# Attention rows split into f16 halves per head and turned by transposing DMAs per pair of heads

## The chip, the core and the metric

The kernel runs on one core of a Trainium2 chip, in one launch. The metric is the device time of one execution in microseconds (us). Differences in this text are differences of that time. The profile is taken from one execution; its engines are PE (TensorE matmul), PEld (TensorE weight load), DVE (VectorE), ACT (ScalarE), POOL (GpSimd) and SP (SyncE, which issues most DMAs).

## What is computed

Two residual blocks on x of shape (4, 1024, 256). The first is a cross attention whose queries are the normalised x and whose keys and values come from the context rows and the normalised x together, with 16 heads of 64 columns; the second is a layer of eight experts of which the best one is taken for each token. Cut to what matters here:

```python
def _L0_xattn_ref(x, latents, ...):
    x = layer_norm(x, ln_m_g, ln_m_b)            # context, (4, 154, 256)
    lat = layer_norm(latents, ln_l_g, ln_l_b)    # (4, 1024, 256)
    q = lat @ Wq
    k, v = jnp.split(jnp.concatenate([x, lat], axis=1) @ Wkv, 2, axis=-1)
    q, k, v = (split_heads(q), split_heads(k), split_heads(v))
    dots = jnp.einsum('bhid,bhjd->bhij', q, k) * scale
    out = jnp.einsum('bhij,bhjd->bhid', jax.nn.softmax(dots, axis=-1), v)
    return out.transpose(0, 2, 1, 3).reshape(b, m, heads * dim_head) @ Wout

x = x + _L0_xattn_ref(ctx_1024, _layernorm(x), ...)
x = x + _L0_ffn_ref(_layernorm(x), ...)          # top-1 of eight experts
```

## The kernel before

**Precision.** Products that need more than f16 are made from halves: a value is kept as an f16 high half and an f16 low half (the value less its high half), and a product is summed from high x high, high x low and low x high.

**Order of work.** The attention part runs over 64 heads, 16 for each of 4 batches. A head h has ten steps j, one for each tile of up to 128 keys (JT = 10). PE's order is written out by hand. At step j it scores the tile that lies three tiles ahead (`tile_ahead`), makes the small chunks that a table places beside the step (`BESIDE`: the next heads' q/k projections "qk", maxima of scores "rest" and "first", their tails, a "turn" of the maxima, values "v", and in some heads the gate "xt" and "gate" of the batch before or the next batch's columns "z"), and weighs the values with the tile's probabilities (`weigh`), which adds up in `acc`. Chunks go through two PSUM banks `aux[0]` and `aux[1]` in turn; a chunk can start when the chunk two before it has been taken by DVE (`aux_done`). The gate chunks lie beside heads 4 to 11 of batches 1, 2 and 3.

**Engines.** ACT makes the exponentials of each scored tile twice, as f32 (`exponent`) and as the f16 high half (`high_half`). POOL makes the low half (`low_half`, L783) for nine of the ten tiles, and in each head also turns a piece of the expert weights into two halves (L792, L795). DVE takes the chunks (`consume`): for a q/k chunk a cast to `raw[0]` (L1059) and a subtraction to `raw[1]` (L1061), for a maximum a reduction (L1077); it also makes the low half of the last tile, on 32 rows (L1152). After the ten steps, `take_rows(h)` divides the sums in `acc` by their denominators (L1139, L1141).

**SP's queue.** All of SP's DMAs leave in program order: per head the stores and the load of the weight piece, `arrange(h + 2)` (the projected q and k are copied to where the scores read them) when the third q/k chunk is done, `send_max(h + 1)` when the "turn" chunk is done, and `arrange_low(h + 2)`.

**The end of a batch.** `att_rows` holds the divided rows of all 16 heads as f32, 128 rows by 8 tiles by 1024 columns. In `put_out(b)` PE turns a tile of 128 rows by eight f32 transposes through a score bank (L1380), ACT casts the turned tile to its high half (L942), DVE subtracts for the low half (L1181), and PE multiplies the tile with `Wout` in 24 products of 256 columns (L1297, pair by pair, three products each). Tile t + 2 is turned behind tile t's products. For tiles 0 and 1 the first seven pairs are turned before the batch's last rows are there. DVE adds the residual rows (L1114) that SP loads into the two `x_res` buffers, tile t + 2's load behind the addition of tile t, and makes the sums of the next norm. In the last batch the gate's chunks for the same batch stand between the tiles.

Of the kernel before, what the change touches and what calls it, by code (L numbers as in the profile page):

```python
# [339 lines left out]
def attention(nc, x, ctx_in, ln, Wq, Wkv, Wout, x2_dram, gate, W1, W2, split_dram):  # L340
# [12 lines left out]
    with stack:  # L353
# [33 lines left out]
        probs_split = [[sb(f"probs_split{h}{i}", [P, N], F16) for i in range(SPLITS)] for h in range(2)]  # L387
# [4 lines left out]
        att_rows = sb("att_rows", [P, NT, H, DH], F32)  # L392

        att_turn = sb("att_cols", [P, 2, 2, INNER // P, P], F16)
        att_cols = [[att_turn[:, h, i, :, :] for i in range(2)] for h in range(2)]
        x_next = att_turn[:, :, :, :, :].rearrange("p a b k t -> p (a b k t)").bitcast(F32)\
# [20 lines left out]
        staging = att_rows[:, :, :, :].rearrange("p t h d -> p (t h d)")  # L417
# [50 lines left out]
        att_turned = sem("att_turned")  # L468
        att_high = sem("att_high")
        att_low = sem("att_low")  # L470
        res_loaded = [sem(f"res_loaded{i}") for i in range(2)]
# [46 lines left out]
        def bank_of(chunk):  # L518
            return aux[NUMBER[chunk] % 2]
# [30 lines left out]
        EARLY = range(PAIRS - 1)  # L550
        PARTS = [EARLY, range(PAIRS - 1, PAIRS)]
        TURNS = NT + 1

        def turn_bank(t, ks):
            return acc if t == 0 and ks != EARLY else score[(t + 1) % 2]

        def turns_of(b, t, part=1):

            return TURNS * b + (part + 1 if t == 0 else t + 2)

        def last_scored(h, i):

            return (h + 1, 2 - i) if h + 1 < HEADS else (h, JT - 2 + i)

        def columns(ks):
            return slice(ks.start * P, ks.stop * P)
# [31 lines left out]
        def _(sp):  # L598
# [14 lines left out]
            sp.dma_start(x_next, x_rows[1]).then_inc(x_loaded[1], 16)  # L613
# [52 lines left out]

            def send_max(g):

                sp.wait_ge(aux_done, NUMBER["turn", g] + 1)
                sp.dma_start(q_max[g % 2][DH:DH + 1, :], max_row[g % 2][:, :]).then_inc(max_sent, 16)  # L670

            def head(h):
                if h > 0:
                    store_piece(h - 1)
                load_piece(h)
                for step in BESIDE[h]:
                    for chunk in step:
                        if chunk == ("qk", h + 2, QK - 1):
                            arrange(h + 2)
                        elif chunk == ("turn", h + 1):  # L680
                            send_max(h + 1)
                if h + 2 < HEADS:
                    arrange_low(h + 2)
                if h % H == 0 and 2 <= h // H + 1 < B:

                    sp.dma_start(x_next, x_rows[h // H + 1]).then_inc(x_again, 16)

            def put_out(b):
                if b == B - 1:
                    store_piece(HEADS - 1)  # L690

                def store(t):
                    sp.wait_ge(aux_done, NUMBER["out", b, t] + 1)
                    sp.dma_start(x2_rows[b, t], x2_keep[:, t, :]).then_inc(x2_stored[t % 2], 16)

                for t in range(NT):
                    if t >= 2:
                        sp.wait_ge(aux_done, NUMBER["out", b, t - 2] + 1)
                    sp.dma_start(x_res[t % 2], x_rows[b, :, t, :]).then_inc(res_loaded[t % 2], 16)
                    if t >= 1:  # L700
# [20 lines left out]
        def _(pool):  # L721
# [64 lines left out]
            for h in range(HEADS):  # L786
                for j in range(JT):
                    low_half(h, j)
                    if j == PIECE_STEPS[0]:
                        pool.wait_ge(piece_loaded, 16 * (h + 1))  # L790
                        at_least(pool, piece_stored, 2 * 16 * h)
                        nc.gpsimd.tensor_copy(piece_out[0][:, :], piece_in[:, :]).then_inc(piece_high, 1)  # L792
                    elif j == PIECE_STEPS[1]:
                        pool.wait_ge(piece_high, h + 1)
                        nc.gpsimd.tensor_tensor(out=piece_out[1][:, :], in0=piece_in[:, :], in1=piece_out[0][:, :],  # L795
                                                op=ALU.subtract).then_inc(piece_low, 1)
# [7 lines left out]
        def _(act):  # L804
# [55 lines left out]
            def normalise_next(b, t):  # L860

                if t == 0:
                    act.wait_ge(inverse_ready, b)
                    if b >= 2:
                        act.wait_ge(x_again, 16 * (b - 1))
# [70 lines left out]
            def put_out(b):  # L936
                for t in range(NT + 2):
                    if t < NT:
                        for part, ks in enumerate(PARTS if t == 0 else [range(PAIRS)]):
                            act.wait_ge(att_turned, turns_of(b, t, part))  # L940
                            act.sem_inc(act_turns, 1)
                            nc.scalar.activation(att_cols[0][t % 2].rearrange("p k t -> p (k t)")[:, columns(ks)],  # L942
                                                 turn_bank(t, ks)[:, columns(ks)], ACT.Copy).then_inc(att_high, 1)
# [14 lines left out]
        def _(dve):  # L958
# [22 lines left out]
            def rows_of(group):  # L981

                return (x_stage[0], x_stage[1], x_next, x_stage[0], x_stage[1])[group], \
                    C_ROWS if group == 0 else [P] * NT
# [148 lines left out]
            def take_rows(h):  # L1133

                for i in range(2):
# [5 lines left out]
                    nc.vector.tensor_tensor(out=att_rows[:, ts, h % H, :], in0=sums[:, :, 0:DH],  # L1141
                                            in1=recip[:, ts].unsqueeze(2).to_broadcast([P, NT // 2, DH]), op=ALU.mult)\
                        .then_inc(rows_taken, 1)

# [29 lines left out]
            def put_out(b):  # L1174
                steps = output_chunks(b)
                for t in range(len(steps) + 1):
                    if t < NT:
                        for part, ks in enumerate(PARTS if t == 0 else [range(PAIRS)]):
                            high, low = [a[t % 2][:, :, :].rearrange("p k t -> p (k t)")[:, columns(ks)] for a in att_cols]
                            dve.wait_ge(att_high, turns_of(b, t, part))  # L1180
                            nc.vector.tensor_tensor(out=low, in0=turn_bank(t, ks)[:, columns(ks)], in1=high,  # L1181
                                                    op=ALU.subtract).then_inc(att_low, 1)
# [28 lines left out]
        def _(pe):  # L1211
# [31 lines left out]
            def produce(chunk):  # L1243
# [44 lines left out]
                elif kind == "out":  # L1288
                    t = chunk[2]
                    parts = PARTS if t == 0 else [range(PAIRS)]  # L1290
                    for part, ks in enumerate(parts):
                        pe.wait_ge(att_low, turns_of(g, t, part))
                        for k in ks:
                            lhs = [a[t % 2][:, k, :] for a in att_cols]
                            rhs = [w[:, k, :] for w in wo]
                            for i, (m, n) in enumerate(((0, 0), (0, 1), (1, 0))):
                                last = nc.tensor.matmul(bank[:, 0:D], lhs[m], rhs[n], start=(k == 0 and i == 0),  # L1297
                                                        stop=(k == PAIRS - 1 and i == 2))
# [15 lines left out]
                last.then_inc(aux_full, 1)  # L1314

# [19 lines left out]
            def weigh(h, j, i):  # L1335
# [3 lines left out]
                if j == 0:  # L1339
                    at_least(pe, rows_taken, 2 * (h - 1) + i + 1)  # L1340
                    if i == 0:
                        pe.wait_ge(aux_done, NUMBER["v", h // 2, len(VALUE_TILES) - 1] + 1)
                r = key_rows(j)
# [16 lines left out]
            def head(h):  # L1360
                for j in range(JT):
# [6 lines left out]
                    if j == JT - 1 and outputs_behind(h) is not None:  # L1368
                        pe.wait_ge(rows_taken, 2 * h)
                        wait_high(pe, *last_scored(h, 1))  # L1370
                        turn_pairs(0, EARLY).then_inc(att_turned, 1)
# [5 lines left out]
            def turn_pairs(t, ks):  # L1377

                for k in ks:
                    last = nc.tensor.transpose(turn_bank(t, ks)[:, k * P:k * P + P], att_rows[:, t, 2 * k:2 * k + 2, :]  # L1380
                                               .rearrange("p h d -> p (h d)"), ident[:, :])
                return last

            def put_out(b):
                pe.wait_ge(w_low, 7)
                h = H * b + H - 1
                wait_high(pe, *last_scored(h, 0))
                turn_pairs(1, EARLY)
                pe.wait_ge(rows_taken, 2 * H * (b + 1))
                turn_pairs(0, PARTS[1]).then_inc(att_turned, 1)  # L1390
                turn_pairs(1, PARTS[1]).then_inc(att_turned, 1)
                for t, step in enumerate(output_chunks(b)):
# [495 lines left out]
```

## Time and profile before

| | |
|---|---|
| Time, median of 3 runs | 2083.61 us (2081.96 to 2087.18) |
| Profiled execution, span from first to last instruction | 2083.0 us |
| Mean granted TensorE clock in it | 0.982 |
| Busy: PE, DVE, ACT, POOL | 1982.6, 1516.5, 1526.0, 1442.8 us |
| DMA packets | 129585, 140.02 MB |

The time of the profiled execution is known by its span; the median of the runs is 0.6 us above it. Busy times of different engines overlap. PE's matmuls are pipelined, so the step from one start to the next tells more than the duration of one.

### The profile page before, as it was taken

The numbers are of one execution on the slowest core, as the hardware profiler recorded it, in microseconds if no ns is written. First come the engines' busy times: TensorE is split into PE (matmuls) and PEld (weight loads), VectorE is DVE, ScalarE is ACT, GpSimd is POOL, SyncE is SP. The second block draws the span as 40 slices with busy tenths as digits, with TensorE's granted clock in tenths as the row PEclk, the third lists the DMA queues.
The fourth block names the chain that finished last, engine by engine and source line by source line (L and its number), as shares of the span: only waits on it lengthen the run. The fifth ranks groups of instructions, "written<-read, shape, count | busy, mean of one in ns | idle before, by whom it ended". The sixth has DMA issues, their size and how long they took to land. (4 is left out here: it accounts for less than half of the span.)

```text
span 2083.0 us, 63335 instructions
## 1 busy us (share of the span) xinstructions
PE 1982.6 (95%) x25468; PEld 1359.6 (65%) x25468; DVE 1516.5 (73%) x2951; ACT 1526.0 (73%) x2006; POOL 1442.8 (69%) x818
## 2 busy tenths in 40 slices
PE   4999999999999999999999999999999998599997
PEld 1566666667666666676666666766666666467775
DVE  8777777776777777777877777777777774745554
ACT  3688888885888787858888888678888886156664
POOL 3688888883888888838888888568888886023332
PEclk8999999999999999999999999999999999799999
DMA  5222222222222222223222222222222221381110
GB/s 190 50 64 59 56 58 68 56 50 78 72 55 56 56 55 56 58 66 76 63 59 55 56 56 55 59 65 66 61 56 55 56 55 32 95 310 39 43 48 25
DMA packets 129585, 140.02 MB, mean 67 GB/s; under 512 B 45569, under 2 KB 94389, under 8 KB 128149
## 3 DMA queue, kind: packets, MB, share of 16 engines
q1 hardware_dynamic: 125557, 126.58, 23.6%
q0 software_dynamic: 3744, 9.39, 1.5%
q8 instruction: 210, 3.44, 0.7%
q14 instruction: 74, 0.61, 0.1%
HBM read 55.15 MB, written 26.15 MB: 39 GB/s over the span
## 5 line engine op out<-in xcount | busy, mean ns | idle before, releaser
L783 POOL TENSOR_TENSOR probs_split<-probs,probs_split 128x1024 f16<-128x1024 f32 x576 | 1221.7, 2134 | 256.1 <-ACT probs_split L890 246.8
L883 ACT ACTIVATE probs<-score 128x1024 f32<-128x1024 f32 (+1 forms) x640 | 655.5, 1024 | 303.6 <-PE score L1240 296.4
L1077 DVE TENSOR_REDUCE max_parts<-aux 128x1 f32<-128x512 f32 x1024 | 682.8, 687 | 79.0 <-PE aux L1240 71.0
L890 ACT ACTIVATE probs_split<-score 128x1024 f16<-128x1024 f32 (+1 forms) x640 | 654.0, 1022 | 0.0
L1352 PE MATMUL acc<-values,probs_split 128*128 128x65 f16 x5120 | 553.8, 193 | 8.2 <-POOL probs_split L783 8.1
L1356 PE MATMUL acc<-values,probs_split 128*128 128x64 f16 x4608 | 519.0, 194 | 0.0
L1357 PE MATMUL acc<-values,probs_split 128*128 128x65 f16 x4608 | 517.0, 192 | 0.0
L1352 PEld LDWEIGHTS acc<-values,probs_split 128*128 128x128 f16 x5120 | 461.4, 97 | 68.3 <-POOL probs_split L783 11.7
L1240 PE MATMUL score<-q_max,k_low 65*128 65x512 f16 (+1 forms) x1280 | 486.6, 380 | 0.0
L1240 PE MATMUL score<-q_both,k_high 128*128 128x512 f16 (+1 forms) x1280 | 483.9, 378 | 0.9 <-DMA q_max<-max_row 0.5
L1240 PE MATMUL aux<-k_high,q_both 128*128 128x512 f16 (+1 forms) x1536 | 457.9, 332 | 19.0 <-DVE max_parts L1077 7.1
L1356 PEld LDWEIGHTS acc<-values,probs_split 128*128 128x128 f16 x4608 | 425.9, 97 | 74.1
L1357 PEld LDWEIGHTS acc<-values,probs_split 128*128 128x128 f16 x4608 | 427.2, 99 | 0.0
L1240 PEld LDWEIGHTS aux<-k_high,q_both 128*128 128x128 f16 x1536 | 141.8, 98 | 156.1 <-DVE max_parts L1077 41.5
L1240 PE MATMUL aux<-zx,wqk 128*128 128x512 f16 x768 | 191.4, 386 | 2.1 <-DVE zx L1027 2.1
L1059 DVE CAST raw<-aux 128x512 f16<-128x512 f32 (+1 forms) x192 | 108.8, 567 | 94.9 <-PE aux L1240 81.6
L1240 PEld LDWEIGHTS score<-q_max,k_low 65*128 65x128 f16 (+1 forms) x1280 | 127.0, 99 | 68.3 <-issue 0.3
L1240 PEld LDWEIGHTS score<-q_both,k_high 128*128 128x128 f16 (+1 forms) x1280 | 129.9, 101 | 62.7 <-issue 1.4
L1810 PE MATMUL up<-shared,w 128*128 128x128 f16 x1872 | 162.7, 223 | 4.4 <-issue 2.1
L1810 PEld LDWEIGHTS up<-shared,w 128*128 x1872 | 131.3, 99 | 53.3 <-issue 17.7
L1583 POOL DMA_INDIRECT out<-shared,write_i x39 | 39.9, 1022 | 168.1 <-DVE shared L1745 168.1
L1617 ACT ACTIVATE shared<-up,b_cols 128x128 f32<-128x128 f32 x312 | 88.9, 368 | 87.9 <-PE up L1810 87.8
(182 smaller groups left out, 2220.2 us busy)
## 6 DMA issues: line engine op xcount, KB each, us to landing
k_high<-raw SPq DMA_DIRECT2D x128, 147.2 KB, 2.5
q_both<-raw SPq DMA_DIRECT2D x128, 128.0 KB, 2.5
piece_in<-in_L_ffn_W SPq DMA_DIRECT2D x64, 256.0 KB, 3.2
halves<-piece_out SPq DMA_DIRECT2D x128, 128.0 KB, 2.4
k_low<-raw SPq DMA_DIRECT2D x64, 147.2 KB, 2.4
q_max<-raw SPq DMA_DIRECT2D x64, 128.0 KB, 2.5
w<-halves SPq DMA_DIRECT2D x16, 512.0 KB, 6.9
w<-halves SPq DMA_DIRECT2D x8, 1024.0 KB, 10.3
```

Source lines behind the costliest of these rows:

```text
L783: nc.gpsimd.tensor_tensor(out=low[0:r, :], in0=prob(h, j)[0:r, :], in1=high[0:r, :], op=ALU.subtract)\
L883: nc.scalar.activation(prob(h, j)[0:r, :], score[j % 2][0:r, :], ACT.Exp, scale=SCALE)\
L890: nc.scalar.activation(halves(h, j)[0][0:r, :], score[j % 2][0:r, :], ACT.Exp, scale=SCALE)\
L1059: nc.vector.tensor_copy(raw[0][:, lo:hi], bank[:, 0:hi - lo]).then_inc(raw_high, 1)
L1077: nc.vector.tensor_reduce(max_parts[g % 2][:, t, c:c + 1], bank[:, :], AX.X, ALU.max)\
L1240: last = nc.tensor.matmul(out, a, b, start=(i == 0), stop=(i == len(pairs) - 1))
L1352: last = nc.tensor.matmul(out, high, value[:, 0:DH + 1], start=(j == 0 and q == 0), stop=(copied and q == NT // 2 - 1))
L1356: nc.tensor.matmul(out[:, 0:DH], high, value[:, DH + 2:VROW], start=False, stop=False)
L1357: last = nc.tensor.matmul(out, low, value[:, 0:DH + 1], start=False, stop=False)
L1583: nc.gpsimd.indirect_dma_start(out=out_rows, out_offset=bass.IndirectOffsetOnAxis(write_i[:, k:k + 1], 0), in_=y_rows[u], in_offset=None, ...
L1617: nc.scalar.activation(hidden[u % 2][:, c * P:c * P + P], up[u % 2][:, c * P:c * P + P], ACT.Silu, bias=b1_cols[:, ds(e * KF + c, 1)]).the ...
L1810: last = nc.tensor.matmul(up[u % 2][:, c * P:c * P + P], lhs, z_split[b][u % 2][:, kk, :], start=(n == 0), stop=(n == 3 * KD - 1))
```

## The change

The f32 store of all heads goes. `att_rows` holds one head. After each head DVE casts its rows to f16 (`att_half`, two heads side by side, 128 x 8 x 128 columns for a pair), and the subtraction for the low half is made by POOL behind its fourth tile of the next head, or by DVE after the last head of a batch. In every even head SP issues, between `arrange` and `send_max`, two transposing DMAs for the pair that is done, one for each half: 128 x 1024 f16 each, turned block by block into `att_cols`, which holds all eight pairs of a batch. The last pair's two are issued at the head of SP's `put_out`. PE's transposes, ACT's casts and DVE's subtractions of `put_out` go.

In `put_out`, PE first multiplies pairs 0 to 6 of tiles 0 to 3 (21 products each), tiles 0 and 1 into the `aux` banks and tiles 2 and 3 into the two halves of `acc`, then waits for the last pair, adds its three products to each of the four tiles, and goes on with tiles 4 to 7 in full.

Buffers that shared memory with the old tiles move: the weight staging lies in `att_cols` now, the rows of batch 1 are read first into `x_second` (in the probabilities' halves, for their statistics) and once more into `x_next` behind head 0.

The diff, cut to its core. `place` and `head` are SP's, the subtraction behind `ATT_STEP` is POOL's, `take_rows` is DVE's, `weigh` and the last `put_out` are PE's.

```diff
-        att_rows = sb("att_rows", [P, NT, H, DH], F32)
-        att_turn = sb("att_cols", [P, 2, 2, INNER // P, P], F16)
+        att_rows = sb("att_rows", [P, NT, DH], F32)
+        att_half = sb("att_half", [P, 2, NT, 2, DH], F16)
+        att_cols = sb("att_cols", [P, PAIRS, 2, NT, P], F16)
...
+        HELD = range(4)
+        IN_ACC = (2, 3)
+        PLACE_STEP = 3
+        ATT_STEP = 3
+        def placed_before(pair):
+            return 2 * 16 * pair
...
+            def place(pair):
+                last = 2 * pair + 1
+                b, k = pair // PAIRS, pair % PAIRS
+                if pair == 0:
+                    sp.wait_ge(w_low, 7)
+                if b > 0 and k == 0:
+                    sp.wait_ge(aux_done, NUMBER["out", b - 1, NT - 1] + 1)
+                for i, made in enumerate((att_high, att_low)):
+                    sp.wait_ge(made, last + 1)
+                    sp.dma_start_transpose(att_cols[:, k, i, :, :],
+                                           att_half[:, i, :, :, :].rearrange("p t h d -> p (t h d)"))\
+                        .then_inc(att_placed, 16)
...
+                    if j == PLACE_STEP and h > 0 and closes_pair(h - 1) and not closes(h - 1):
+                        place(h // 2 - 1)
...
-                if h % H == 0 and 2 <= h // H + 1 < B:
+                if h % H == 0 and h // H + 1 < B:
+                    if h == 0:
+                        sp.wait_ge(var_ready, B + 1)
                     sp.dma_start(x_next, x_rows[h // H + 1]).then_inc(x_again, 16)
             def put_out(b):
+                place(PAIRS * (b + 1) - 1)
...
+                    if j == ATT_STEP and h > 0 and not closes(h - 1):
+                        pool.wait_ge(att_high, h)
+                        nc.gpsimd.tensor_tensor(out=att_of(1, h - 1), in0=att_rows[:, :, :], in1=att_of(0, h - 1),
+                                                op=ALU.subtract).then_inc(att_low, 1)
...
             def take_rows(h):
+                at_least(dve, att_low, h)
                 for i in range(2):
...
-                    nc.vector.tensor_tensor(out=att_rows[:, ts, h % H, :], in0=sums[:, :, 0:DH],
+                    nc.vector.tensor_tensor(out=att_rows[:, ts, :], in0=sums[:, :, 0:DH],
...
+                dve.wait_ge(rows_taken, 2 * (h + 1))
+                at_least(dve, att_placed, placed_before(h // 2))
+                nc.vector.tensor_copy(att_of(0, h), att_rows[:, :, :]).then_inc(att_high, 1)
+                if closes(h):
+                    dve.wait_ge(att_high, h + 1)
+                    nc.vector.tensor_tensor(out=att_of(1, h), in0=att_rows[:, :, :], in1=att_of(0, h),
+                                            op=ALU.subtract).then_inc(att_low, 1)
...
             def weigh(h, j, i):
+                        if h > 0 and closes(h - 1):
+                            pe.wait_ge(aux_done, NUMBER["out", h // H - 1, IN_ACC[-1]] + 1)
...
             def put_out(b):
                 pe.wait_ge(w_low, 7)
-                turn_pairs(1, EARLY)
-                pe.wait_ge(rows_taken, 2 * H * (b + 1))
-                turn_pairs(0, PARTS[1]).then_inc(att_turned, 1)
-                turn_pairs(1, PARTS[1]).then_inc(att_turned, 1)
+                pe.wait_ge(att_placed, placed_before(PAIRS * (b + 1) - 1))
+                for t in HELD:
+                    if t in IN_ACC:
+                        pe.wait_ge(rows_taken, 2 * H * (b + 1))
+                    else:
+                        at_least(pe, aux_done, NUMBER["out", b, t] - 1)
+                    weigh_out(b, t, EARLY)
+                pe.wait_ge(att_placed, placed_before(PAIRS * (b + 1)))
...
-                        if chunk[0] == "out" and t + 2 < NT:
-                            turn_pairs(t + 2, range(PAIRS)).then_inc(att_turned, 1)
```

## Rows read from the trace of the kernel before

**Rows 1.** The page's first line.

```profile
span 2083.0 us, 63335 instructions
```

**Rows 2.** Windows: us, busy time (instructions) by engine, granted clock, DMA share.

```profile
core 0: us, PE busy (x) PEld busy (x) DVE busy (x) ACT busy (x) POOL busy (x), PEclk, DMA share, GB/s
550.00:600.00 50.00, 49.70 (x683) 33.22 (x682) 39.72 (x72) 40.99 (x46) 44.79 (x25) 1.00 0.25 58
```

**Rows 3.** Timeline at the end of batch 0, PE, then DVE: start, us, engine, group.

```profile
465.34 0.95 PE L1380 MATMUL score<-ident,att_rows 128*128 128x128 f32 x7
...
469.61 2.78 PE L1297 MATMUL aux<-wo,att_cols 128*128 128x256 f16 x24 [0.65 <-DVE att_cols L1181]
472.22 1.04 PE L1380 MATMUL score<-ident,att_rows 128*128 128x128 f32 x8
473.10 2.78 PE L1297 MATMUL aux<-wo,att_cols 128*128 128x256 f16 x24
...
472.42 0.42 DVE L1114 TENSOR_TENSOR x_keep<-aux,x_res 128x256 f32<-128x256 f32 x1 [1.01 <-PE aux L1297]
```

**Rows 4.** Timeline of DVE at an ordinary border between heads.

```profile
547.63 0.42 DVE L1141 TENSOR_TENSOR att_rows<-acc,recip 128x256 f32<-128x256 f32 x1
547.97 0.68 DVE L1077 TENSOR_REDUCE max_parts<-aux 128x1 f32<-128x512 f32 x1
548.78 0.69 DVE L1059 CAST raw<-aux 128x512 f16<-128x512 f32 x1
```

**Rows 5.** Timeline of DVE at a border after a gate head.

```profile
724.93 0.42 DVE L1141 TENSOR_TENSOR att_rows<-acc,recip 128x256 f32<-128x256 f32 x1
...
726.49 0.69 DVE L1059 CAST raw<-aux 128x512 f16<-128x512 f32 x1 [0.54 <-PE aux L1240]
```

**Rows 6.** Timeline of PEld and of PE at the ordinary border.

```profile
550.24 1.11 PEld L1240 LDWEIGHTS aux<-zx,wqk 128*128 128x128 f16 x6 [0.19 <-DVE raw L1061]
...
550.39 1.46 PE L1240 MATMUL aux<-zx,wqk 128*128 128x512 f16 x6
```

**Rows 7.** POOL: two groups (busy, mean ns, idle before), then its timeline at both borders.

```profile
L783 POOL TENSOR_TENSOR probs_split<-probs,probs_split 128x1024 f16<-128x1024 f32 x576 | 1221.7, 2134 | 256.1 <-ACT probs_split L890 246.8
...
L795 POOL TENSOR_TENSOR piece_out<-piece_in,piece_out 128x512 f16<-128x512 f32 x64 | 74.1, 1158 | 0.0
...
545.90 4.38 POOL L783 TENSOR_TENSOR probs_split<-probs,probs_split 128x1024 f16<-128x1024 f32 x2 [0.23 <-ACT probs_split L890]
...
723.10 4.38 POOL L783 TENSOR_TENSOR probs_split<-probs,probs_split 128x1024 f16<-128x1024 f32 x2 [0.30 <-ACT probs_split L890]
```

**Rows 8.** Groups of instructions: DVE casts from SBUF of two widths.

```profile
L1700 DVE CAST read_i<-owner 128x39 int32<-128x39 f32 x1 | 0.2, 183 | 0.0
...
L1653 DVE CAST counts_i<-counts 128x8 int32<-128x8 f32 x1 | 0.2, 170 | 0.0
```

**Rows 9.** Line L1152 (ns min/median/max), then DVE and POOL around one of its instructions.

```profile
L1152 DVE TENSOR_TENSOR probs_split<-probs,probs_split x64: 1216/1217/2411, 89.2 to 1750.0; 32x1024 f16<-32x1024 f32 x64
...
515.61 1.92 DVE L1152 TENSOR_TENSOR probs_split<-probs,probs_split 32x1024 f16<-32x1024 f32 x1 [0.79 <-ACT probs_split L890]
...
514.33 2.12 POOL L783 TENSOR_TENSOR probs_split<-probs,probs_split 128x1024 f16<-128x1024 f32 x1
```

**Rows 10.** Timeline of SP and PE in one head, then the page's DMA issues.

```profile
734.94 1.27 SPq L658 DMA_DIRECT2D k_high<-raw  x2
738.44 0.70 SPq L670 DMA_DIRECT2D q_max<-max_row  x1
...
742.17 0.38 PE L1240 MATMUL score<-q_both,k_high 128*128 128x512 f16 x1
...
piece_in<-in_L_ffn_W SPq DMA_DIRECT2D x64, 256.0 KB, 3.2
...
x_res<-in_x SPq DMA_DIRECT2D x32, 128.0 KB, 2.5
...
k_high<-raw SPq DMA_DIRECT2D x128, 6.5 KB, 2.0
```

More of the change, by code:

```diff
@@ L386, in attention @@
         probs = [sb(f"probs{i}", [P, N], F32) for i in range(PROBS)]
-        probs_split = [[sb(f"probs_split{h}{i}", [P, N], F16) for i in range(SPLITS)] for h in range(2)]
+        probs_halves = sb("probs_split", [P, 2, SPLITS, N], F16)
+        probs_split = [[probs_halves[:, h, i, :] for i in range(SPLITS)] for h in range(2)]
+        x_second = probs_halves[:, 0, :, :].rearrange("p i c -> p (i c)").bitcast(F32)\
+            .rearrange("p (t d) -> p t d", d=D)
         values = [sb(f"values{i}", [P, 2, JT, VROW], F16) for i in range(2)]
         recip = sb("recip", [P, NT], F32)
-        att_rows = sb("att_rows", [P, NT, H, DH], F32)
-        att_turn = sb("att_cols", [P, 2, 2, INNER // P, P], F16)
-        att_cols = [[att_turn[:, h, i, :, :] for i in range(2)] for h in range(2)]
-        x_next = att_turn[:, :, :, :, :].rearrange("p a b k t -> p (a b k t)").bitcast(F32)\
+        att_rows = sb("att_rows", [P, NT, DH], F32)
+        att_half = sb("att_half", [P, 2, NT, 2, DH], F16)
+        att_cols = sb("att_cols", [P, PAIRS, 2, NT, P], F16)
+        x_next = att_cols[:, PAIRS - 2:PAIRS, :, :, :].rearrange("p k a t c -> p (k a t c)").bitcast(F32)\
             .rearrange("p (t d) -> p t d", d=D)
@@ L415, in attention @@
         eps_square = sb("eps_square", [P, 1], F32)
-        staging = att_rows[:, :, :, :].rearrange("p t h d -> p (t h d)")
+        staging = att_cols[:, :, :, :, :].rearrange("p k a t c -> p (k a t c)").bitcast(F32)
         w_stage = [staging[:, i * KD * N:(i + 1) * KD * N] for i in range(2)]
@@ L467, in attention @@
         rows_taken = sem("rows_taken")
-        att_turned = sem("att_turned")
         att_high = sem("att_high")
         att_low = sem("att_low")
+        att_placed = sem("att_placed")
         res_loaded = [sem(f"res_loaded{i}") for i in range(2)]
@@ L518, in bank_of @@
         def bank_of(chunk):
+            if chunk[0] == "out" and chunk[2] in IN_ACC:
+                i = IN_ACC.index(chunk[2])
+                return acc[:, i * HALF:i * HALF + HALF]
             return aux[NUMBER[chunk] % 2]
@@ L545, in whole_program, with closes, closes_pair, att_of @@
                     put_out(outputs_behind(h))
[L550 to L566, printed above, removed]
+        EARLY, LATE = range(PAIRS - 1), range(PAIRS - 1, PAIRS)
+        HELD = range(4)
+        IN_ACC = (2, 3)
+        PLACE_STEP = 3
+        ATT_STEP = 3
+        def closes(h):
+            return h % H == H - 1
+        def closes_pair(h):
+            return h % 2 == 1
+        def att_of(i, h):
+            return att_half[:, i, :, h % 2, :]
+        def placed_before(pair):
+            return 2 * 16 * pair
         def z_columns(b, i):
@@ L612, in _ @@
                 load_weight(i)
-            sp.dma_start(x_next, x_rows[1]).then_inc(x_loaded[1], 16)
+            sp.dma_start(x_second, x_rows[1]).then_inc(x_loaded[1], 16)
             load_weight(2)
@@ L675, in head @@
                 load_piece(h)
-                for step in BESIDE[h]:
+                for j, step in enumerate(BESIDE[h]):
                     for chunk in step:
@@ L863, in normalise_next @@
                     act.wait_ge(inverse_ready, b)
-                    if b >= 2:
-                        act.wait_ge(x_again, 16 * (b - 1))
+                    act.wait_ge(x_again, 16 * b)
                 nc.scalar.activation(x_next[:, t, :], x_next[:, t, :], ACT.Identity, scale=rstd[:, b + 1, t:t + 1],
@@ L937, in put_out @@
                 for t in range(NT + 2):
[L938 to L943, printed above, removed]
                     if t == POWERS_TILE and b >= 1:
@@ L981, in rows_of @@
             def rows_of(group):
-                return (x_stage[0], x_stage[1], x_next, x_stage[0], x_stage[1])[group], \
+                return (x_stage[0], x_stage[1], x_second, x_stage[0], x_stage[1])[group], \
                     C_ROWS if group == 0 else [P] * NT
@@ L1176, in put_out @@
                 for t in range(len(steps) + 1):
[L1177 to L1182, printed above, removed]
                     if t >= 1:
@@ L1289, in produce @@
                     t = chunk[2]
[L1290 to L1298, printed above, removed]
+                    if t not in HELD:
+                        weigh_out(g, t, EARLY)
+                    last = weigh_out(g, t, LATE)
                 elif kind == "turn":
@@ L1314, in produce, with weigh_out @@
                 last.then_inc(aux_full, 1)
+            def weigh_out(b, t, ks):
+                bank = bank_of(("out", b, t))
+                for k in ks:
+                    lhs = [att_cols[:, k, i, t, :] for i in range(2)]
+                    rhs = [w[:, k, :] for w in wo]
+                    for i, (m, n) in enumerate(((0, 0), (0, 1), (1, 0))):
+                        last = nc.tensor.matmul(bank[:, 0:D], lhs[m], rhs[n], start=(k == 0 and i == 0),
+                                                stop=(k == PAIRS - 1 and i == 2))
+                return last
             def scores(h, j, i):
@@ L1367, in head @@
                             produce(BESIDE[h][j][i])
[L1368 to L1371, printed above, removed]
                     for i in range(2):
@@ L1375, in head @@
                             produce(BESIDE[h][j][2 + i])
[L1377 to L1382, printed above, removed]
             def put_out(b):
                 pe.wait_ge(w_low, 7)
-                h = H * b + H - 1
-                wait_high(pe, *last_scored(h, 0))
-                turn_pairs(1, EARLY)
-                pe.wait_ge(rows_taken, 2 * H * (b + 1))
-                turn_pairs(0, PARTS[1]).then_inc(att_turned, 1)
-                turn_pairs(1, PARTS[1]).then_inc(att_turned, 1)
-                for t, step in enumerate(output_chunks(b)):
+                pe.wait_ge(att_placed, placed_before(PAIRS * (b + 1) - 1))
[6 more added lines that the diff above has]
+                pe.wait_ge(att_placed, placed_before(PAIRS * (b + 1)))
+                for step in output_chunks(b):
                     for chunk in step:
                         produce(chunk)
-                        if chunk[0] == "out" and t + 2 < NT:
-                            turn_pairs(t + 2, range(PAIRS)).then_inc(att_turned, 1)
             for chunk in BEFORE:
```

## The prediction

> **What bounds the kernel now.** I read the page first: its span is 2083.0 us [rows 1]. The same view cut into windows then shows what fills it. In fifty microseconds in the middle of a batch PE is busy 49.70 us at the full granted clock, DVE 39.72 and POOL 44.79 [rows 2]. PE works nearly without a gap, so a microsecond taken from PE is a microsecond won, and one for which PE is made to wait is lost; a microsecond saved on ACT is worth nothing.
>
> Next I read PE's timeline at the end of batch 0 [rows 3]. The first row group of transposes stands ahead of the last weighing, then every tile of the projection takes 2.61 us of products (24 in 2.61 us: 0.109 us each) and 0.88 us of transposes, a step of 3.49 us. This is the part that the change shortens.
>
> Last I read the border between two heads, on four engines, because that is where the change adds work. DVE takes the rows of the head that ends, then a maximum, then the cast of the next head's first q/k chunk [rows 4]. There it has no idle time in 36 of the 60 borders that lie inside a batch; in the other 24 (after a head that carries a gate chunk, heads 4 to 11 of batches 1 to 3) it waits 0.54 us [rows 5]. PE's next q/k chunk waits for what DVE makes of that cast: its weight load sits 0.19 us until DVE's subtraction (raw) lets it go and starts at 550.24, its product at 550.39, with no gap behind the product before it [rows 6]. The 0.15 us between the two are all that PE has in hand there; I take 0.12. Whatever is put between the rows and that cast reaches PE almost in full.
>
> **The put_out stage: a gain of 20 us.** In batch 0 the last product of the projection ends at 469.61 + 6 x 3.49 + 2 x 2.61 = 495.8 [rows 3] (the last two tiles have no transposes behind them). Without the seven transposes at 465.34 the last weighing, about 0.5 us, is over at 465.8. Then come 4 x 21 held products, 84 x 0.109 = 9.15 us, to 475.0. The last pair has to be there by then: DVE has its rows some 2 us after the last weighing (a maximum and the two divisions lie ahead), cast and subtraction take about 1.5 us, and with two issues and the 3.2 us to landing of the 256 KB row [rows 10] the second transfer lands near 474 (an estimate). I take no wait. The twelve remaining products of the held tiles are short (0.33 us a tile), so DVE and the residual rows become late next: x_res has two buffers, the load for tile 2 is issued only when tile 0 is added (0.42 us after its product [rows 3]) and lands 2.5 us later [rows 10]. Tile 2 is added about 4.0 us after 475.0, and tile 4 needs its bank then. Four tiles of 2.61 follow: 475.0 + 4.1 + 10.4 = 489.5. The gain is 6.2 us a batch, 18.7 for three. Bounds: 9.0 a batch if x_res were no wait, 4 if the pair lands 2 us late. In the last batch xt and gate chunks stand between the tiles and hang on DVE's sums, so the head start of the held tiles is given back; two transposing groups of 0.88 go. I take 1.5 (0 to 6). ACT's and DVE's copies of the turned tiles go too and are worth nothing by themselves. Sum: 20 us, 12 to 33.
>
> **POOL's subtraction: nothing.** One more 128x512 subtraction a head, 1.16 us as the one that it makes of the weight piece; POOL waits 256 us in all ahead of its 576 low halves [rows 7], and the rows it waits for are ready when its fourth tile is done. Without this cover it would cost up to 60 x 1.16 = 70 us.
>
> **DVE's cast, 60 times.** It reads 128x512 f32 from SBUF and writes f16. No row has this shape. The 128x512 cast from PSUM takes 0.69 us [rows 4], the upper bound. SBUF casts are quicker: 0.170 us for 8 columns and 0.183 for 39 [rows 8], 0.42 ns a column, which gives 0.38 us for 512; the PSUM cast, with the same 0.17 us at its start, takes 1.03 ns a column. So the SBUF cast handles about two columns where the other handles one. I take 0.42. The new wait for the rows' own completion costs about 0.04 us and the 0.08 us by which the maximum overlaps the multiply [rows 4]. The maximum thus starts at 548.43 instead of 547.97, the cast of the chunk at 549.08 instead of 548.78, 0.30 later, and PE loses 0.30 - 0.12 = 0.18 us. 36 x 0.18 = 6.5 us; by the upper bound 36 x 0.45 = 16 and 2 for the other 24, whose 0.54 us swallow the short cast.
>
> **The lock between DVE and POOL: 42 us.** DVE's subtraction on 32 rows, which reads two SBUF operands, takes 1.217 us in the median and 2.411 at most [rows 9]. In one of the longer ones DVE starts at 515.61 while POOL is in a low half from 514.33 to 516.45; DVE ends at 517.53, just 1.217 us after 516.31. It had waited for POOL's whole instruction but its last 0.14 us. A cast at that pace has to read SBUF twice where the other reads once, so I take it to wait in the same way; no row shows a wide SBUF cast beside POOL. The Trainium skill states this rule (SBUF — State Buffer, Who interferes with whom): a copy or cast in a two-port mode and a GpSimd instruction exclude each other for the whole instruction, whoever starts first. The page agrees with the 1.92 us row; by it the term below holds, without it the term is nothing and the sum would be 2070.
>
> So what POOL does at the cast decides. I set the two beside each other in all 60 borders. POOL's second low half of the pair starts at 545.90 + 4.38 - 2.13 = 548.15 in an ordinary border, and the cast could start at 547.63 + 0.42 + 0.04 = 548.09: DVE is first by 0.06 us, in 35 of the 36. After a gate head POOL starts at 723.10 + 4.38 - 2.13 = 725.35 and the cast at 724.93 + 0.42 + 0.04 = 725.39: POOL is first by 0.02 to 0.04 us, in 23 of the 24 [rows 4, 5, 7]. There DVE waits until 727.34, 1.95 us. With the 0.46 of an unhindered cast, less DVE's 0.54 and PE's 0.12, PE loses 1.75 us a time: 24 x 1.75 = 42 us. Behind the waiting cast stand the maximum and both halves of the chunk; PE waits for them, ACT for PE. Bounds: 0 (DVE always first) and 42 + 36 x 1.95 = 112 (POOL always first). I take the middle because the order of starts is what rows show.
>
> **The transfers: nothing.** SP issues them behind arrange, whose last two issues end at 734.94 + 1.27 = 736.21, and ahead of send_max, issued at 738.44 when the row of maxima is made; PE needs it at 742.17 [rows 10]. A small transfer lands in 2.0 us, so send_max may go out at 740.1 and the two transfers have 3.9 us of SP and queue. Issues here take 0.6 to 0.7 us and 256 KB land in 3.2. No row has a transposing transfer. Taken like the 256 KB row they cost nothing; if each holds the queue for all of its 3.2 us, send_max lands at 744.6 and PE waits 2.4 us, 28 times (7 pairs in 4 batches): 68 us. The next even head's cast waits for them only at its end, some 10 us later. x_next is read a second time for batch 1, behind head 0, under heads that need no transfer then.
>
> **Sum.** -20 + 6.5 + 42 = +28.5 on the profiled 2083.0, which is 0.6 below the median of the runs, 2083.6: 2112 us.
>
> **Rivals.**
> (a) POOL first everywhere. The 0.06 us by which DVE leads in 36 borders is eaten by the second added wait ahead of the cast. Then 36 x 1.95 = 70 us more: 2182. For it: 0.06 is less than one wait may cost. Against: both sides hang on PE, and the offset is the same to 0.01 us in each border.
> (b) The other side: DVE is first in the 24 too, or the cast takes no lock. Place: the same 24 borders; it decides at 0.04 us of lead. Then 2083.6 - 20 + 6.5 = 2070, faster.
> (c) The cast runs at the pace of the PSUM cast (0.69 us) and without a lock: 2083.6 - 20 + 18 = 2082, no change.
> (d) The transposing transfers hold the queue: from 1.9 us each on PE waits for send_max. With 3.2 us each and no lock 2083.6 - 20 + 6.5 + 68 = 2138. The Trainium skill prices a 128x128 block turned by DMA at 1309 ns (VectorE: DVE Perf Modes, The three transpose paths); eight in a row would be an estimated 10.5 us, far past that point, and no run here shows it.
>
> **Chances.** The forecast 0.32, (a) 0.22, (b) 0.28, (c) 0.08, (d) 0.10. The forecast's own range is 2096 to 2130: the put_out gain of 12 to 33, the casts at 4 to 16. Over all cases I give 2062 to 2188; it holds most of (b), whose put_out bounds reach 2057, and (a) without its end. A measurement of this kernel tells 0.3% (6 us) from no change. Faster by more: most of (b) and a quarter of (c), 0.27. Within: the rest of (b), half of (c) and the edge of the forecast, 0.10. Slower: 0.63.
>
> **What would show it.** The new cast in take_rows: 0.4 us after an ordinary head and 2.4 after a gate head would be the forecast, 2.4 everywhere (a), 0.4 everywhere (b), 0.69 (c). PE idle ahead of a q/k chunk with DVE's raw as releaser, some 50 us in all. Batch tiles 2.61 us apart from tile 4 on, tile 4 waiting for x_keep. PE's score of tile 0 waiting for q_max in even heads alone would be (d). I am wrong if PE is not held by DVE at the border after all, or if a transfer takes more than 6 us, when DVE's wait for it at the end of the even head would hold up everything.

## The result: 2124.1 us, 1.9% slower

The changed kernel takes 2124.1 us in the median of 4 runs (2121.59 to 2130.05) against 2085.39 for the kernel before on the same chip: a ratio of 1.0191 [1.0177, 1.0204]. The prediction was 2112 in a range of 2062 to 2188. The profiled execution has a span of 2123.1, 40.1 above [rows 1]; the terms below are made against that.

**The cast of the rows.** One line over all 64 heads (nanoseconds, least, median and most, then first and last start):

```profile
L1170 DVE CAST att_half<-att_rows x64: 426/427/2384, 96.4 to 1796.6; 128x512 f16<-128x512 f32 x64
```

At least half of them take 0.43 us, the longest 2.38. DVE's timeline at the two borders that answer to [rows 4] and [rows 5], first the ordinary one and then one after a gate head:

```profile
548.63 0.42 DVE L1165 TENSOR_TENSOR att_rows<-acc,recip 128x256 f32<-128x256 f32 x1
549.09 0.43 DVE L1170 CAST att_half<-att_rows 128x512 f16<-128x512 f32 x1
549.43 0.68 DVE L1100 TENSOR_REDUCE max_parts<-aux 128x1 f32<-128x512 f32 x1
550.03 0.68 DVE L1082 CAST raw<-aux 128x512 f16<-128x512 f32 x1
...
705.72 0.42 DVE L1165 TENSOR_TENSOR att_rows<-acc,recip 128x256 f32<-128x256 f32 x1
706.18 2.38 DVE L1170 CAST att_half<-att_rows 128x512 f16<-128x512 f32 x1
708.48 0.68 DVE L1100 TENSOR_REDUCE max_parts<-aux 128x1 f32<-128x512 f32 x1
```

And POOL's low half that lies beside each cast, which answers to [rows 7]:

```profile
549.15 2.36 POOL L809 TENSOR_TENSOR probs_split<-probs,probs_split 128x1024 f16<-128x1024 f32 x1
...
706.14 2.13 POOL L809 TENSOR_TENSOR probs_split<-probs,probs_split 128x1024 f16<-128x1024 f32 x1
```

At the first border DVE starts 0.06 us ahead of POOL: the cast takes 0.43, and it is POOL that runs 2.36 instead of 2.13. At the second POOL starts 0.04 us ahead: its low half ends at 706.14 + 2.13 = 708.27, and the cast at 708.56, so that its own 0.43 began at 708.13, 1.95 us late. POOL is first at 23 of the 24 gate borders, at 22 of them by 0.03 to 0.04 us and at one (760.60) by 0.40. At the last (head 56, where the cast starts at 1620.79) DVE is first by 0.09 and the cast takes 0.43. There the period of the head, from its rows to the next head's, is 25.07 us as before; after the other even gate heads it is mostly 26.72. (In the kernel before, the one gate border at which DVE would have been first was another, head 36.)

The wait reaches PE behind the maximum and behind the chunk's halves, here at the second border:

```profile
709.21 0.39 PE L1265 MATMUL aux<-k_high,q_both 128*128 128x512 f16 x1 [0.80 <-DVE max_parts L1100]
710.54 1.47 PE L1265 MATMUL aux<-zx,wqk 128*128 128x512 f16 x6 [0.50 <-DVE raw L1084]
```

**PE at the end of batch 0**, which answers to [rows 3]: start, us, products, and in brackets the wait ahead and its releaser.

```profile
476.30 4.75 PE L1342 MATMUL acc<-wo,att_cols 128*128 128x256 f16 x42
480.88 0.82 PE L1342 MATMUL aux<-wo,att_cols 128*128 128x256 f16 x6
481.89 0.50 PE L1342 MATMUL acc<-wo,att_cols 128*128 128x256 f16 x3 [0.19 <-DVE x_keep L1137]
482.89 0.50 PE L1342 MATMUL acc<-wo,att_cols 128*128 128x256 f16 x3 [0.50 <-DVE x_keep L1137]
485.46 12.32 PE L1342 MATMUL aux<-wo,att_cols 128*128 128x256 f16 x96 [2.07 <-DVE x_keep L1137]
```

PE goes from the 84 held products into the last pair's without a wait, so the pair is there in time. Then it waits for DVE's additions, 2.07 us ahead of tile 4, and DVE waits for the residual rows:

```profile
484.98 0.42 DVE L1137 TENSOR_TENSOR x_keep<-acc,x_res 128x256 f32<-128x256 f32 x1 [1.47 <-DMA x_res<-in_x]
```

The 96 products of tiles 4 to 7 take 12.32 us in place of 10.65. Windows show why (columns as in [rows 2]; the granted clock is the third number from the end):

```profile
484.00:485.40 1.40, 0.00 (x0) 0.00 (x0) 0.42 (x1) 0.00 (x0) 0.00 (x0) 1.00 0.67 223
485.40:486.40 1.00, 0.94 (x9) 0.85 (x10) 0.93 (x4) 0.28 (x1) 0.00 (x0) 1.00 0.12 42
486.40:487.40 1.00, 1.00 (x10) 0.77 (x8) 0.61 (x3) 0.29 (x2) 0.00 (x0) 0.70 0.40 128
487.40:489.40 2.00, 2.00 (x11) 1.44 (x10) 0.00 (x0) 0.01 (x1) 0.00 (x0) 0.50 0.57 178
489.40:490.40 1.00, 1.00 (x7) 0.74 (x6) 0.80 (x2) 0.00 (x0) 0.00 (x0) 0.59 0.06 16
490.40:492.00 1.60, 1.60 (x17) 1.43 (x16) 0.23 (x2) 0.29 (x1) 0.00 (x0) 1.00 0.26 82
```

PE was idle for 2.7 of the 4.4 us from 481 to 485.4. It resumes at a granted clock of 1.00; then the clock falls to the lower level (1.2 GHz) for some 3 us, with PE fully busy. Eleven products take 2.0 us there.

**SP** in an even head, and the page's line on the transfers, which answer to [rows 10]:

```profile
718.72 2.70 SPq L685 DMA_TRANSPOSE att_cols<-att_half  x2
721.46 0.70 SPq L692 DMA_DIRECT2D q_max<-max_row  x1
...
att_cols<-att_half SPq DMA_TRANSPOSE x64, 3.3
```

An issue takes 1.33 us in the median, about twice the 0.6 to 0.7 of the plain ones beside it, and the 256 KB land in 3.3, near the 3.1 of a plain row of that size in the same run.

**Where the 40.1 us went.** The start of DVE's second division in each head gives the head's period. The differences to the kernel before, in us, summed by kind:

| | predicted | profile |
|---|---|---|
| 24 periods that begin with a gate border | 42 | 39.0 (1.63 each) |
| 32 other periods inside the batches | 6.5 | 12.4 |
| ends of batches 0, 1, 2 (last head's period and put_out) | -18.7 | -5.0, -6.5, -1.9 |
| end of the last batch, to the end of the span | -1.5 | +2.2 |
| sum | 28.3 | 40.1 |

The prediction rounded the put_out gain to 20 and so came to 28.5; its 6.5 was counted over 36 borders, four of which fall into the ends here.

### The profile page after: what moved, and what is told of

Read it like the earlier page. It is cut to its first block and busy times, and to the rows that moved or that the text cites. A ratio compares the mean times of both kernels' runs of the same rounds, so it can differ in the third digit from the quotient of the medians.

```text
span 2123.1 us, 63009 instructions
## 1 busy us (share of the span) xinstructions
PE 1971.1 (93%) x25212; PEld 1324.5 (62%) x25212; DVE 1556.0 (73%) x2983; ACT 1496.8 (71%) x1970; POOL 1522.4 (72%) x878
## 5 line engine op out<-in xcount | busy, mean ns | idle before, releaser
L912 ACT ACTIVATE probs<-score 128x1024 f32<-128x1024 f32 (+1 forms) x640 | 655.4, 1024 | 356.4 <-PE score L1265 326.0
L1265 PE MATMUL aux<-zx,wqk 128*128 128x512 f16 x768 | 192.0, 387 | 13.6 <-DVE raw L1084 11.5
## 6 DMA issues: line engine op xcount, KB each, us to landing
w<-halves SPq DMA_DIRECT2D x8, 1024.0 KB, 10.5
```

Of the source, the lines that this page charges most:

```text
L912: nc.scalar.activation(prob(h, j)[0:r, :], score[j % 2][0:r, :], ACT.Exp, scale=SCALE)\
L1265: last = nc.tensor.matmul(out, a, b, start=(i == 0), stop=(i == len(pairs) - 1))
```

## The experiments

Ratios are against the kernel before on the same chip (2084.7 beside experiments 1 to 4, 2084.9 beside 5 to 8). The first 100 us of an execution vary by a few microseconds (last section), so sums over the heads' periods, made as in the table, stand beside the medians.

**1. The cast on ACT.**

```diff
-                nc.vector.tensor_copy(att_of(0, h), att_rows[:, :, :]).then_inc(att_high, 1)
...
+                    if j == CAST_STEP and h > 0 and not closes(h - 1):
+                        act.wait_ge(rows_taken, 2 * h)
...
+                        nc.scalar.activation(att_of(0, h - 1), att_rows[:, :, :], ACT.Copy).then_inc(att_high, 1)
```

> The cast of the rows goes from DVE to ACT, behind ACT's two exponentials of step 0 of the next head. Theory (the cast and its wait for POOL cost the time): the 24 gate borders give back 39 us and the 32 ordinary periods of the rows shown give back 12, 2124 - 51 = 2073, which is 10 below the kernel before; the period of a gate head goes from 26.72 back to 25.07, that of an ordinary head from 24.87 to 24.48. Rival 1 (the ordinary heads lose their 0.39 us to the transposing transfers or to POOL's added subtraction): only the 39 come back, 2085. Rival 2 (ACT has no room): up to 0.6 us a head comes back as waiting for ACT, about 2073 + 36 = 2109, with PE idle behind ACT's or POOL's probs_split.

The cast stands in ACT's `head`, with `CAST_STEP = 0`; the last head of a batch keeps it on DVE. Measured: 2081.7, ratio 0.9981 [0.9971, 0.9990]. The gate periods are 1.1 us over those of before (39.0 in the changed kernel), the others 5.4 (12.4). ACT's 60 casts cost it 38.6 us and nobody waits for them:

```profile
L947 ACT ACTIVATE att_half<-att_rows 128x512 f16<-128x512 f32 x60 | 38.6, 644 | 0.0
```

So 37.9 of the 39.0 us of gate loss and 7.0 of the 12.4 go with DVE's cast: rival 2 falls, and rival 1 can hold for the 5.4 us that stay. The theory had 51 us coming back; the medians show 42.4. Not all of the 7.0 is the cast itself: in these periods PE's waits for q_max fall from 4.5 us in the changed kernel to 2.2 here. Of the remaining 5.4, one head shows a cause plainly (PE's timeline):

```profile
1425.45 0.38 PE L1270 MATMUL score<-q_both,k_high 128*128 128x512 f16 x1 [1.60 <-DMA q_max<-max_row]
```

**2. The high half from PSUM.**

```diff
...
+                    by = recip[:, ts].unsqueeze(2).to_broadcast([P, NT // 2, DH])
+                    nc.vector.tensor_tensor(out=att_of(0, h)[:, ts, :], in0=sums[:, :, 0:DH], in1=by, op=ALU.mult)
...
-                nc.vector.tensor_copy(att_of(0, h), att_rows[:, :, :]).then_inc(att_high, 1)
```

> DVE makes the high half by two more multiplies from PSUM (0.42 us each) in place of the cast from SBUF (0.43). Theory (only an instruction of DVE whose operands all lie in SBUF waits for POOL): no multiply is longer than 0.43 us. DVE's work at the border grows by 0.84 us against before: ordinary heads lose about 0.7 us, 36 x 0.7 = 25, gate heads 0.25, 24 x 0.25 = 6; with the put_out gain of 11 that is 2083.6 - 11 + 31 = 2103. Rival (any DVE instruction that writes f16 to SBUF waits for POOL): some of the new multiplies take 1.9 us or more and the time stays at 2124 or above.

Measured: 2093.95, ratio 1.0041 [1.0026, 1.0055]. The gate periods lose 1.1 us in all, the others 16.5; the 31 us expected were too many. Not one of the 128 new multiplies waits, although 125 of them lie wholly beside a low half of POOL:

```profile
L1168 DVE TENSOR_TENSOR att_half<-acc,recip x128: 414/414/417, 97.9 to 1766.9; 128x256 f16<-128x256 f32 x128
```

Same engine, same place, same output, and DVE works 0.4 us longer there; the source is PSUM, and two multiplies stand in for one cast. The rival falls. Which of the two differences frees them from POOL, this run alone doesn't tell.

**3. Four buffers for the residual rows** (the changed kernel otherwise).

```diff
...
+        x_more = sb("x_more", [P, 2 * D], F32)
-        x_res = [x_both[:, i * D:i * D + D] for i in range(2)]
+        x_res = [x_of[:, i * D:i * D + D] for x_of in (x_both, x_more) for i in range(2)]
...
```

> Four buffers for the residual rows in place of two, tiles 0 to 3 loaded at once. Theory (PE's wait of 2.07 and 2.59 us ahead of tile 4 in batches 0 and 2 is the load of tile 2, and the granted clock falls behind that wait): tile 4 starts 1.6 us earlier in batch 0, 0.3 in batch 1, 1.6 in batch 2, and the clock stays at 1.0 behind it, 1.4 to 1.9 us in each of two batches: 2124 - 7 = 2117. Rival (the short products of the held tiles bring the clock down, however long the wait is): 2124 - 3.5 = 2120, with the granted clock at 0.5 in the same place.

Measured: 2123.3, ratio 1.0176 [1.0155, 1.0196]. The end of batch 0 gains 3.2 us against the changed kernel, of batch 1 0.2, of batch 2 1.7; the profile's end of the last batch is 2.9 longer and its first head's rows come 2.2 later, and the median, above both 2117 and 2120, doesn't tell it from the changed kernel. Tile 4 starts 1.6, 0.3 and 1.6 us earlier, as expected. The clock does only half of what the theory says: it stays up in batch 0 and falls in batch 2. PE at the end of batch 1, where it stays up too, then of batch 2:

```profile
925.02 0.50 PE L1351 MATMUL acc<-wo,att_cols 128*128 128x256 f16 x3 [1.01 <-DVE x_keep L1146]
926.52 10.65 PE L1351 MATMUL aux<-wo,att_cols 128*128 128x256 f16 x96 [0.99 <-DVE x_keep L1146]
...
1366.55 0.50 PE L1351 MATMUL acc<-wo,att_cols 128*128 128x256 f16 x3 [1.00 <-DVE x_keep L1146]
1368.05 12.32 PE L1351 MATMUL aux<-wo,att_cols 128*128 128x256 f16 x96 [1.00 <-DVE x_keep L1146]
```

Behind the same waits the clock fell in batch 2 and not in batch 1. So the load of tile 2 is not the whole of it: the clock can fall behind waits of 1 us too, and whether it does differs from one batch to the next. Neither the theory nor the rival says why.

**4. The cast one maximum later.**

```diff
...
+                            consume(chunk)
+                            if cast:
+                                cast_rows(h - 1)
...
```

> DVE's cast comes one maximum (0.69 us) later, behind the first chunk of the next head. Theory (whoever starts first holds the other off for its whole instruction): POOL's low half is now under way at the ordinary borders too. The cast there takes about 1.9 us instead of 0.43 and 36 borders lose some 1.4 us more, 50 us; at the gate borders it takes 1.7 and ends when it did: 2174. Rival (POOL holds DVE off only where both start within a few hundredths of a microsecond, or for a reason of the gate heads): the cast stays at 0.43 in ordinary borders, and the time at 2124 or below.

Measured: 2158.4, ratio 1.0351 [1.0334, 1.0369]. The cast's median goes from 0.427 to 1.99 us:

```profile
L1159 DVE CAST att_half<-att_rows x64: 426/1991/2116, 98.9 to 1831.8; 128x512 f16<-128x512 f32 x64
```

The 32 ordinary periods lose 54.2 us against the kernel before, 1.5 to 1.6 in most of them, and the casts there start 0.4 us behind POOL's low half and end 0.28 behind its end: what the gate heads lost was the order of starts, and nothing that the gate heads do. The total is below the 2174 expected mainly because the gate periods lose less than in the changed kernel, 26.2 in place of 39.0. There the maximum no longer stands behind the waiting cast, which fits the 0.6 us less in each; no run separates it.

**5. The transfers behind send_max** (with the cast on ACT, as in 6 to 8).

```diff
-        PLACE_STEP = 3
+        PLACE_STEP = 5
...
```

> The kernel with ACT's cast (2081.7), and SP issues the two transposing transfers behind send_max in place of ahead of it. Theory (what the ordinary heads still lose, 5.4 us, is send_max held back by the two issues of 1.33 us: PE waits 1.60 us for q_max in one head and a few tenths in others): 3 to 4 us come back, 2078. Rival (the rest is ACT's and POOL's added work, which the place of the transfers doesn't touch): 2081.7, the same heads longer.

Measured: 2077.4, ratio 0.9967 [0.9956, 0.9979]. PE's wait for q_max, 2.8 us in experiment 1, is gone from the page's line for the score, and the 32 periods are 3.0 over those of before in place of 5.4.

```profile
L1270 PE MATMUL score<-q_both,k_high 128*128 128x512 f16 (+1 forms) x1280 | 484.0, 378 | 1.1 <-ACT probs_split L920 0.8
```

**6. Only the waits that the banks need**, and four residual buffers.

```diff
...
-                at_least(pe, aux_done, number - 1)
...
+                if kind == "out" and g < B - 1 and chunk[2] < 6:
+                    if chunk[2] >= 4:
+                        pe.wait_ge(aux_done, number - 3)
+                else:
+                    at_least(pe, aux_done, number - 1)
...
```

> The kernel with ACT's cast (2081.7), four buffers for the residual rows, and in batches 0 to 2 PE waits for a bank only where the bank was really in use: tiles 2 and 3 not at all, tile 4 for the addition of tile 0, tile 5 for that of tile 1. Theory (the put_out gain is short of the forecast 6.2 us a batch by these waits and by the clock that falls behind them): tile 4 follows 1.3 us behind the 84 held products, 3.3, 3.0 and 4.3 us earlier than in the changed kernel, and 24 products at half clock (1.7 us) go in two batches: 2081.7 - 14 = 2068. Rival (DVE's additions and sums are the bound of this part, 1.03 us a tile, and the waits only move to tiles 6 and 7; or the clock falls all the same): half of it, 2075.

Measured: 2066.75, ratio 0.9919 [0.9902, 0.9935]. PE at the end of batch 2, where the changed kernel had waited 2.59 us and lost the clock:

```profile
1323.89 0.82 PE L1360 MATMUL aux<-wo,att_cols 128*128 128x256 f16 x6
1324.54 0.82 PE L1360 MATMUL acc<-wo,att_cols 128*128 128x256 f16 x6
1325.20 10.78 PE L1360 MATMUL aux<-wo,att_cols 128*128 128x256 f16 x96
```

No wait, and 96 products in 10.78 us. The clock stays at 1.00 in batches 0 to 2. The three ends gain 10.2, 9.7 and 8.0 us against the kernel before, more than the 6.2 forecast, since tile 4 no longer waits for tile 2. Against experiment 3, which has the four buffers but the old waits, they gain 2.0, 2.9 and 4.4.

**7. All of it**, and two held tiles in the last batch (`HELD = [range(4)] * (B - 1) + [range(2)]`).

> ACT's cast, transfers behind send_max, four residual buffers, PE's waits as in the run before, and in the last batch two held tiles in place of four. If the gains add up: 2068 - 3.5 - 2.5 = 2062, 1.1 per cent below the kernel before. If the last batch doesn't gain by fewer held tiles (its transposes of the gate wait for the chain of DVE and ACT behind each tile in any case): 2064.

Measured: 2061.47, ratio 0.9893 [0.9877, 0.9910]. This is 1.1% below the kernel before. From the last head's rows to the end of the span it takes 2.7 us less than experiment 6.

**8. Two held tiles everywhere** (the cast on ACT and nothing else).

> The kernel with ACT's cast (2081.7) and two held tiles in place of four in every batch: 42 products in place of 84 ahead of the wait for the last pair. Theory A (DVE's low half of the last pair waits for POOL, 2.50 us, and the second transfer lands some 7 us behind the rows): PE waits about 4 us behind the 42 products in batches 0 to 2; the waits for the residual rows, 2 to 3 us, go in return; the last batch gains 2: 2081.7 + 3 x 1.5 - 2 = 2084. Theory B, as the prediction put it (the pair lands some 3 us behind the 42 products and DVE's additions are then the bound): the middle batches are unchanged or quicker, 2077.

Measured: 2078.94, ratio 0.9974 [0.9965, 0.9984]. PE at the end of batch 0, with the first of its 42 held products at 469.70:

```profile
477.62 0.83 PE L1347 MATMUL aux<-wo,att_cols 128*128 128x256 f16 x6 [3.17 <-DMA att_cols<-att_half]
478.63 5.41 PE L1347 MATMUL acc<-wo,att_cols 128*128 128x256 f16 x48 [0.19 <-DVE x_keep L1142]
483.88 10.64 PE L1347 MATMUL aux<-wo,att_cols 128*128 128x256 f16 x96
```

The pair is there 7.9 us behind the first held product. Theory A has the landing right, and B comes nearer to the time: against experiment 1 the ends of batches 0 to 2 are 2.2 us shorter in all, because the waits for the residual rows go for the 3.1 to 3.2 us that PE waits here, and the end of the last batch is 4.3 shorter. In batch 1, where the clock falls behind a wait of 3.09 us, the end is 1.1 longer; in batches 0 and 2 it stays up behind 3.17 and 3.11.

## Why the prediction was right, and where it was off

**The lock, right.** The cast at DVE's place waits for POOL's instruction if POOL starts first, and POOL waits if DVE does; 0.04 us of lead decided it as forecast, in 22 of 24 gate borders, and 0.40 us in one more. Forecast 1.75 us a time, measured 1.63 over all 24 and 1.70 over the 23 at which the cast waits; the forecast had read 23 and priced 24. Experiment 4 turned the order at the other borders and so made most of rival (a). Experiments 1 and 2 took the lock away and with it the loss. Rival (b), DVE first or no lock, was false at this place; without the lock the kernel reaches 2081.7 and not 2070, for the reasons of the last two points below. The Trainium skill's rule (SBUF — State Buffer, Who interferes with whom) agrees with the 1.95 us that the cast waits at 706.18 and with the 0.23 us by which POOL's low half is longer at 549.15. The same section says that an instruction of DVE with two inputs in SBUF contends with a GpSimd instruction that reads SBUF, and that one with at most one, outside the two-port modes, does not; the traces agree: DVE's closing subtraction takes 2.50 us in batches 0 to 2 and 0.69 in the last, where POOL has stopped, and the multiplies of experiment 2, with one input in PSUM, take 414 to 417 ns.

```profile
L1173 DVE TENSOR_TENSOR att_half<-att_rows,att_half x4: 691/2496/2497, 473.9 to 1797.0; 128x512 f16<-128x512 f32 x4
```

**The cast itself, right in duration.** 0.42 forecast, 0.427 measured, rival (c) is out. The part of the other periods that goes when ACT casts is 12.4 - 5.4 = 7.0, against 6.5. That these agree so well is in part luck, since about 2.4 us of the 7.0 are waits for q_max, which the forecast put at nothing.

**The transfers at nothing, too low.** The step was "the two transfers have 3.9 us of SP and queue". The room is there in most heads, and the landing in 3.3 us is that of a plain row, so rival (d) in its size is out, and the 10.5 us estimated there with it. But two issues take 2.7 us rather than 1.3, and where the transfer's own waits come late, send_max is late: PE waits 4.5 us for q_max in the 32 periods of the changed kernel, and 2.4 us of the 5.4 that experiment 1 left go with the transfers' place. What is left, some 3 us (0.15 in many odd heads, 1.2 in one of the last), stays open.

**The put_out gain, mis-sized: 20 forecast, 11.3 measured, just under its lower bound of 12.** The 84 held products (9.17 us) were right, and the pair was in time: 8.2 us behind the last weighing by the forecast, 7.8 in batch 0 (7.9 in experiment 8). That number came out by luck: DVE's subtraction waits for POOL, so that cast and subtraction take 3.0 us and not 1.5, and the sum added two issues ahead of the landing, of which the first lies under the subtraction and the second is part of the 3.1 us to landing. Tile 4's start was nearly right in two batches: 4.1 us behind the held products forecast, 4.58 measured in batch 0, 4.32 in batch 1, but 5.61 in batch 2. What failed is "four tiles of 2.61 follow". In batches 0 and 2 the clock fell behind the waits, 12.32 us for 96 products where 10.65 is the full-speed figure, and in batch 2 the wait was 2.59. Batch 2 also loses 0.9 us behind its last product, from there to the next head's rows; that stays open. In the last batch the step "the head start of the held tiles is given back" was too kind: PE waits 2.78 and 1.42 us for the gate's rows behind the held tiles, and 24 products at the lower clock (0.50 granted from 1813 to 1817) take 5.11 us. Experiment 6 shows that the forecast gain was there to be had. With experiment 3 it shows that neither the residual loads alone nor DVE's pace set it, but also waits written for a bank order that the held tiles don't have; the new waits with two buffers were not run.

One of the signs it named, 50 us of PE idle with raw as releaser, came out smaller and for the most part under another name: at the 23 gate borders PE waits 18.6 us for the maximum behind the cast and 11.5 for raw, 30.1 of the 39.0, and for neither in the kernel before. How the rest of the 39.0 reaches PE was not traced.

## What to carry to other kernels

Where two engines can hold each other off, set their starts side by side before adding an instruction: 0.04 us of order decided 1.6 us a time here. The same work on a third engine cost 6.5 us over the gate and other periods, and from PSUM 17.6, in place of 51.4. Work that is held ahead of a wait needs the waits behind it rewritten too: an "n minus 2" rule made for two banks in turn cost 2.0 to 4.4 us a batch (experiment 6 against 3) once two of the tiles lay elsewhere. A short idle time of PE is priced at itself and at the clock that may fall behind it, 1.7 us for 96 products here.

## What was not expected of the hardware

The fall of the clock behind waits of 1 us is not a rule: with the same three waits (0.19, 1.00, 1.00) it fell in one batch and not in another (experiment 3), and with 3.09 to 3.17 us in one of three batches (experiment 8). A transposing transfer of 256 KB is as quick as a plain one (3.3 us to 3.1), though the packets under 512 B went from 45569 to 113169. And the first 100 us differ between executions: from 60 to 80 us the granted clock was 1.00 in the profiles before and after and in those of experiments 5 to 7, 0.74 in 1 to 3 and 0.83 in 4 and 8, whose first head's rows come 1.9 to 3.7 us later, whatever was changed.
